# A graph network on one Trainium2 core: operands of VectorE moved to PSUM, the target comparison moved to ScalarE, and a memset behind each gather of GpSimd

## The chip, the core and the metric

The kernel is one program on one core of a Trainium2 chip. The metric is the device time of one execution in microseconds (us), the median of the runs shown. The profiled execution is a run of its own.

## What is computed

Two graph layers over 3125 nodes of 256 values and 53125 edges that are sorted by their target node (`dst`). Each layer is added to its input; each works on `h = relu(layernorm(x))`.

```
# first layer: attention over the edges, 4 heads of rank 16
ZU     = einsum('nd,kdr->knr', Z, U)
logits = (ZU[:, src] * ZU[:, dst]).sum(-1) / 4
exp_l  = exp(logits - segment_max(logits, dst)[dst])
alpha  = exp_l / (segment_sum(exp_l, dst)[dst] + 1e-16)
agg    = segment_sum(alpha[..., None] * ZU[:, src], dst)
ssa    = einsum('k,knr,kdr->nd', softmax(head_w), agg, U)
Z_half = 0.5 * Z + 0.5 * ssa
out    = relu(Z_half + 0.5 * ((Z_half - Z_half @ Dmat.T @ Dmat) @ Dmat) - 0.05)
# second layer: messages summed at their targets, then a GRU cell
red    = segment_sum(h[src] + relvectors[edge_type], dst)
out    = gru_cell(red, h)
```

## The kernel before

The nodes are cut into 25 windows of 125 (`NW`, `W`). The edges into one window lie together, and each window reads a span of 18 tiles of 128 edges (`C`), the edge on the partition. A set-up stage finds where each window's edges begin, makes ZU for all nodes and stores it as a table of 64 values a row in HBM (`zu_table`). The first layer then runs the windows one after another with the body of `attend` written out 25 times on each engine (`overlapped`); the second layer (`gru`) runs on the result and has no gather. The order on each engine is the order in which the code is written, and semaphores alone tie the engines together.

One window `t` of the first layer, `h = t % 2` being the half of each double buffer:

- **GpSimd** (`gather`, L638) fetches the source rows of ZU: 18 indirect DMAs, one for each tile of 128 edges, into `zs[h]`, in three chunks of 8, 8 and 2 tiles that count on semaphores of their own. The offsets are `sidx[:, h, :]`, which VectorE copied from `src_col` (`sources`, L963) once it was done with the same half two windows before. For the first two windows GpSimd copies them itself (L646).
- **SyncE** (`prefetch`) loads the targets of window `t + 2`, the same 2304 of them on each of 125 partitions, into `dst_bc[h]`, behind `oht_made`.
- **VectorE** multiplies the source rows with the target rows in PSUM (`logits`, L954) and sums over the rank (L957), chunk by chunk. Between the chunks it finishes the rows of window `t - 1`: `renew` (L1057 to L1066) and `shift` (L1071). Then it takes the maximum of each run of edges with the same target by two scans (L995, L997, L1001), makes the one-hots of the targets of window `t + 1` (`target_one_hots`, L924: `dst_bc` compared with the node number of the partition, written as bf16 to `ohT`), the remainder of the rows (L915), the difference of logits and maximum (`dif`, L1008), three bf16 parts of the target rows of `t + 1` (`split_rows`, L929 to L937), the weighted rows `V` (L1013: `zs` times the exponentials, both in SBUF), the offsets of window `t + 2` (L963), the cuts between runs (L941), the edge one-hots of `t + 1` (`one_hots`, L892: `iota_w` plus the window's first node compared with `dst_col`, both in SBUF) and a third of the finished rows (L919). When the sums of window `t` are there it divides by the denominators (`weigh`, L1038 on, whose instruction L1038 is the first of VectorE after TensorE's sums) and copies the transposed means (L1052).
- **ScalarE** does for window `t - 1` the logarithm and exponential of the layer norm, the rows `h2s` (L1404) and their first bf16 part (L1375), then for window `t` the copy of the transposed row (`keep_turned`, L1357), the exponential of `dif` straight into the columns `V[:, :, KR:KR + K]` (L1334, semaphore `P_made`), and afterwards the second bf16 part (L1380), the cuts (L1326), the counts (L1362) and the next dense row (L1352).
- **TensorE** transposes the logits (L1609) and the maxima (L1612), does a dense part (L1637), then makes the target rows of window `t + 1` from `ohT` and the three bf16 parts, 54 matmuls of 128x64 (`target_rows`, L1600), then the sums of window `t`, 18 fp32 matmuls (L1623, shown as 36), and last the transposed means and the product with them (L1641, L1643). `target_rows` waits for `oht_made` and for the five steps of `split_rows`.

Every engine has a second way through the kernel for graphs that do not fit the windows (`by_blocks`); it is not taken with these inputs and the change leaves it alone.

Of the kernel before, what the change touches and what calls it, by code (L numbers as in the profile page):

```python
# [24 lines left out]
def gnn_kernel(nc, x, edges, U, Dmat, head_w, rel, w_ih, w_hh, b_ih, b_hh, out):  # L25
# [5 lines left out]
    K, _, R = U.shape  # L31
    KR = K * R
# [23 lines left out]
    with ctx:  # L56
# [177 lines left out]
        any_top = sb("any_top", [W, 1])  # L234
        most_e = sb("most_e", [128, C * K])
# [127 lines left out]
        V_made = sem("V_made")  # L363
        agg_made = sem("agg_made")
# [9 lines left out]

        sidx_made = [sem(f"sidx_made{h}") for h in range(2)]
# [231 lines left out]
        def _(pool):  # L607
# [24 lines left out]
            def gather(i, h, table, to, done):  # L632

                pool.wait_ge(sidx_made[h], i + 1)
                pool.nop(nofuse=True)
                for c, (a, b) in enumerate(CHUNKS):
                    for j in range(a, b):
                        nc.gpsimd.indirect_dma_start(  # L638
                            out=to(h, j), out_offset=None, in_=table,
                            in_offset=bass.IndirectOffsetOnAxis(ap=sidx[:, h, j:j + 1], axis=0),  # L640
                        ).then_inc(done[h][c], 16)

            def windowed():
                pool.wait_ge(a_col, 1)
                for h in range(2):
                    nc.gpsimd.tensor_copy(sidx[:, h, :], src_col[:, h, :]).then_inc(sidx_made[h], 1)  # L646
                pool.wait_ge(st_zu, 16 * 5)
                each_window(lambda t, i, h: gather(
                    i, h, zu_table, lambda h, j: zs[h][:, j * KR:(j + 1) * KR], g_zs))
# [74 lines left out]
        def _(dve):  # L724
# [162 lines left out]
            def one_hots(t, h):  # L887

                in0 = iota_w[:, 0:W].unsqueeze(1).broadcast_to([128, C, W])
                col = flat(dst_col[:, :, :], t, C).unsqueeze(2).broadcast_to([128, C, W])  # L890
# [90 lines left out]
            def attend(t, i, h, first, last):  # L981
# [20 lines left out]
                ahead = (t + 1, i + h, 1 - h)  # L1002
                if not last:
                    target_one_hots(*ahead)
                if not first:
                    remainder(t - 1, 1 - h)
                dve.wait_ge(mT_made, t + 1)
# [805 lines left out]
```

## Time and profile before

| what | value |
|---|---|
| runs | 1218.30, 1241.45, 1218.26 us; median 1218.3 us |
| profiled execution | 1217.22 us, of which the profile's span is 1215.6 us |
| mean granted TensorE clock | 0.704 of full speed |
| busy in the span | PE 853.1 us (70%), DVE 682.5 us (56%), ACT 293.9 us (24%), POOL 563.5 us (46%) |
| 180 to 360 us | PE 118.59, DVE 108.06, ACT 27.85, POOL 142.82 us busy of 180; granted clock 0.50 |
| 405 to 760 us | PE 217.79, DVE 196.93, ACT 50.07, POOL 282.51 us busy of 355; granted clock 0.50 |

The span is that of one execution, from the first instruction to the last. PE is TensorE, DVE VectorE, ACT ScalarE, POOL GpSimd, SP SyncE. In a timeline each line gives the start, the duration, engine, line of the kernel, operation, tiles and shapes, and in brackets how long the engine sat idle before it and what ended that; "issue" is time in which it waited for nothing that the profile shows. The two stretches of the last two rows are both inside the windows of the first layer.

### The profile page before, as it was taken

The numbers are of one execution on the slowest core, as the hardware profiler recorded it, in microseconds if no ns is written. First come the engines' busy times: TensorE is split into PE (matmuls) and PEld (weight loads), VectorE is DVE, ScalarE is ACT, GpSimd is POOL, SyncE is SP. The second block draws the span as 40 slices with busy tenths as digits, with TensorE's granted clock in tenths as the row PEclk, the third lists the DMA queues.
The fourth block names the chain that finished last, engine by engine and source line by source line (L and its number), as shares of the span: only waits on it lengthen the run. The fifth ranks groups of instructions, "written<-read, shape, count | busy, mean of one in ns | idle before, by whom it ended". The sixth has DMA issues, their size and how long they took to land.

```text
span 1215.6 us, 14336 instructions
## 1 busy us (share of the span) xinstructions
PE 853.1 (70%) x5247; PEld 640.5 (53%) x5247; DVE 682.5 (56%) x1264; ACT 293.9 (24%) x621; POOL 563.5 (46%) x495
## 2 busy tenths in 40 slices
PE   0451656667655666665556666569999999999997
PEld 0341444456544455544445555446666666676764
DVE  4452566664565664455556555545566666555562
ACT  5230111111111111111111111224333333344331
POOL 3537277787778787777787877300000000000000
PEclk9985655555555555555555555569999999999999
DMA  4226233334333333332333331000000000000000
GB/s 126 79 48 128 81 72 69 73 79 95 73 70 71 73 81 82 78 68 68 71 71 74 80 84 35 12 13 18 17 15 16 13 18 17 18 17 18 18 14 14
DMA packets 42545, 65.97 MB, mean 54 GB/s; under 512 B 14247, under 2 KB 31696, under 8 KB 39350
## 3 DMA queue, kind: packets, MB, share of 16 engines
q1 hardware_dynamic: 24843, 48.23, 12.0%
q0 software_dynamic: 16576, 16.76, 11.0%
q8 instruction: 42, 0.69, 0.3%
q14 instruction: 28, 0.23, 0.1%
q10 hardware_dynamic: 1056, 0.07, 0.1%
HBM read 57.69 MB, written 7.20 MB: 53 GB/s over the span
## 4 chain that ended last, share of the span: by engine, by line
POOL 42%; PE 35%; issue 13%; DVE 4%; SPq 3%; DMA 2%; ACT 1%; POOLq 0%; DVEq 0%; ACTq 0%
POOL shared L638 40%; PE bank L1671 11%; PE bank L1670 5%; PE bank L1714 4%; PE bank L1721 4%; PE bank L1655 3%; PE bank L1722 2%; PE bank L1715 2%; DVE layer L1076 1%; DVE layer L1078 1%; POOL oh L712 1%; PE bank L1519 1%; PE bank L1682 1%; DMA layer<-in_edges,row_at 1%; DMA rels<-in_L_gnn_relvectors 1%
## 5 line engine op out<-in xcount | busy, mean ns | idle before, releaser
L638 POOL DMA_INDIRECT shared<-zu_table,sidx x450 | 534.5, 1188 | 162.9 <-issue 136.5
L1623 PE MATMUL bank<-layer,oh 128*125 128x84 f32 x900 | 192.1, 412 | 0.0
L1623 PEld LDWEIGHTS bank<-layer,oh 128*125 128x125 f32 x900 | 187.9, 326 | 0.0
L1600 PE MATMUL bank<-zu,shared 125*128 125x64 bf16 x1350 | 85.3, 238 | 78.8 <-issue 43.5
L1600 PEld LDWEIGHTS bank<-zu,shared 125*128 125x128 bf16 x1350 | 74.7, 127 | 102.4 <-issue 102.3
L1038 DVE TENSOR_SCALAR den<-bank 125x4 f32<-125x4 f32 x25 | 4.1, 162 | 189.9 <-issue 129.7
L1609 PE MATMUL bank<-ident,L 128*72 128x128 f32 x75 | 21.0, 417 | 125.6 <-DVE L L957 68.8
L1076 DVE COPY layer<-bank 125x256 f32<-125x256 f32 x25 | 10.6, 424 | 141.0 <-PE bank L1671 141.0
L907 DVE TENSOR_TENSOR shared<-iota_b,key_col 128x3125 bf16<-128x3125 bf16 x25 | 85.2, 3409 | 0.0
L907 DVE TENSOR_TENSOR oh<-iota_b,low_col 128x3125 bf16<-128x3125 bf16 x25 | 85.2, 3409 | 0.0
L1609 PEld LDWEIGHTS bank<-ident,L 128*72 128x72 f32 x75 | 9.4, 159 | 135.6 <-DVE L L957 73.8
L1362 ACT ACTIVATE cnt_rows<-meansT 51x125 bf16<-51x125 f32 x25 | 7.6, 305 | 281.7 <-issue 175.7
L1655 PEld LDWEIGHTS bank<-shared,oh 128*125 128x125 bf16 x625 | 61.7, 142 | 23.9 <-issue 10.0
L1655 PE MATMUL bank<-shared,oh 128*125 128x125 bf16 x625 | 66.5, 225 | 10.0 <-issue 9.0
L1671 PE MATMUL bank<-wide,zus 125*125 125x512 bf16 x208 | 73.3, 389 | 0.0
L1392 ACT ACTIVATE zus<-bank 125x500 bf16<-125x500 f32 (+1 forms) x91 | 60.3, 688 | 41.8 <-PE bank L1655 41.8
L1392 ACT ACTIVATE shared<-bank 125x500 bf16<-125x500 f32 (+1 forms) x84 | 55.8, 685 | 50.3 <-PE bank L1655 50.3
L1671 PE MATMUL bank<-wide,shared 125*125 125x512 bf16 x192 | 65.6, 379 | 0.0
L892 DVE SCALAR_TENSOR_TENSOR oh<-iota_w,win_first,dst_col 128x2250 f32<-128x2250 f32 x25 | 63.8, 2552 | 0.0
L954 DVE TENSOR_TENSOR layer<-shared,bank 128x512 f32<-128x512 f32 (+1 forms) x75 | 41.2, 549 | 37.1 <-DMA shared<-zu_table,sidx 33.3
L1670 PE MATMUL bank<-wide,zus 125*125 125x256 bf16 x195 | 54.3, 278 | 0.0
L1714 PE MATMUL bank<-whhT,layer 128*125 128x512 f32 x100 | 51.1, 593 | 0.0
(227 smaller groups left out, 1513.4 us busy)
## 6 DMA issues: line engine op xcount, KB each, us to landing
shared<-in_edges SPq DMA_DIRECT2D x25, 1125.0 KB
shared<-zu_table,sidx POOLq DMA_INDIRECT x450
xs<-in_x SPq DMA_DIRECT2D x5, 625.0 KB
h_table<-h2s SPq DMA_DIRECT2D x25, 125.0 KB
h2s<-h_table SPq DMA_DIRECT2D x25, 125.0 KB
out_dram<-layer SPq DMA_DIRECT2D x25, 125.0 KB
halo_i<-in_edges SPq DMA_DIRECT2D x25, 108.6 KB
zu_table<-zus SPq DMA_DIRECT2D x5, 156.2 KB
```

What stands on the lines that cost most here:

```text
L638: nc.gpsimd.indirect_dma_start(out=to(h, j), out_offset=None, in_=table, in_offset=bass.IndirectOffsetOnAxis(ap=sidx[:, h, j:j + 1], axis= ...
L892: nc.vector.scalar_tensor_tensor(o, in0, win_first[:, bass.ds(t, 1)], col, ALU.add, ALU.is_equal).then_inc(oh_made, 1)
L907: nc.vector.tensor_tensor(to.rearrange("p (g w) -> p g w", g=BW), io, col[:, t * BW:(t + 1) * BW].unsqueeze(2).broadcast_to([128, BW, W]), ...
L954: nc.vector.tensor_tensor(prod[:, a * KR:b * KR], zs[h][:, a * KR:b * KR], ps(c, 128, 0, (b - a) * KR), ALU.mult).then_inc(prod_made, 1)
L1392: nc.scalar.activation(many[t % 2].rearrange("p (a g d) -> p g a d", a=NW, g=BW)[:, a:b, :, :], ps((7, 1)[g % 2], W, 0, (b - a) * W).rearr ...
L1600: last = mm(ps(c, 128, (j - a) * KR, (j - a + 1) * KR), ohT[:, j * 128:(j + 1) * 128], zu3[:, m, :], start=m == 0, stop=m == 2)
L1623: last = mm(ps(5, W, 0, SUMS), oh[:, h, j * W:(j + 1) * W], V[:, j, :], start=j == 0, stop=j == C - 1)
L1655: last = mm(ps((7, 1)[g % 2], W, (k - a) * W, (k - a + 1) * W), lows[t % 2][:, k * W:(k + 1) * W], keys[t % 2][:, k * W:(k + 1) * W], star ...
L1670: mm(ps(0, W, 0, D), own, v[:, 2, :], start=False, stop=False)
L1671: last = mm(ps(0, W, 0, 2 * D), own, v[:, 0:2, :].rearrange("p m d -> p (m d)"), start=a == 0, stop=a == NW - 1)
L1714: mm(ps(rzb, W, 0, 2 * D), h2T[:, c * W:(c + 1) * W], whhT[:, c, 0:2 * D], start=False, stop=False)
L1721: mm(ps(rzb, W, 0, 2 * D), redT[:, c * W:(c + 1) * W], wihT[:, c, 0:2 * D], start=False, stop=c == CH - 1)
```

## The change

- The exponential of `dif` is made twice on ScalarE: first into PSUM (bank 4, columns 128 to 199), which VectorE's product L1013 now reads, then into `V` as before, for TensorE, under a new semaphore `P_kept`. VectorE's next `dif` and TensorE's sums wait for it.
- `one_hots` reads the targets of the window from PSUM (bank 3, columns 384 to 401), where ScalarE copies them (`targets`) after the exponentials. Window 0 still reads `dst_col` in SBUF.
- `target_one_hots` leaves VectorE. ScalarE makes it with two activations over 125x2304: the absolute difference of target and node, in place in `dst_bc`, and `relu(1 - that)` into `ohT`. In window `t` they stand behind `keep_turned(t)` and ahead of the exponentials.
- GpSimd takes the offsets from `src_col` directly; `sidx`, its semaphores, VectorE's copy L963 and GpSimd's two copies are gone from this way. Before the gathers of window `t` (from 2 on) it waits for `V` of window `t - 2`.
- Behind each gather GpSimd writes zeros to a tile of 128x64 (`idle`), which nothing reads; each of these memsets waits for the one before it.

```diff
+        idle = sb("idle", [128, 64])
...
-            def gather(i, h, table, to, done):
-
-                pool.wait_ge(sidx_made[h], i + 1)
-                pool.nop(nofuse=True)
+            def source_rows(t, i, h):
+
+                if t % GRP == 0:
+                    pool.wait_ge(a_col, 3 * (t // GRP) + 1)
+                if t >= 2:
+                    pool.wait_ge(V_made, t - 1 + CREDIT)
                 for c, (a, b) in enumerate(CHUNKS):
                     for j in range(a, b):
                         nc.gpsimd.indirect_dma_start(
-                            out=to(h, j), out_offset=None, in_=table,
-                            in_offset=bass.IndirectOffsetOnAxis(ap=sidx[:, h, j:j + 1], axis=0),
-                        ).then_inc(done[h][c], 16)
+                            out=zs[h][:, j * KR:(j + 1) * KR], out_offset=None, in_=zu_table,
+                            in_offset=bass.IndirectOffsetOnAxis(ap=src_col[:, t, j:j + 1], axis=0),
+                        ).then_inc(g_zs[h][c], 16)
+                        pool.wait_ge(c_pool, t * C + j + 1)
+                        nc.gpsimd.memset(idle[:, :], 0.0).then_inc(c_pool, 1)
...
             def one_hots(t, h):
-                col = flat(dst_col[:, :, :], t, C).unsqueeze(2).broadcast_to([128, C, W])
+                if t:
+                    dve.wait_ge(targets_made, t)
+                    col = ps(3, 128, 3 * 128, 3 * 128 + C)
+                else:
+                    col = dst_col[:, 0, :]
+                col = col.unsqueeze(2).broadcast_to([128, C, W])
...
-            def target_one_hots(t, i, h):
-                dve.wait_ge(l_bc[h], 16 * (i + 1))
-                nc.vector.tensor_scalar(ohT, dst_bc[h], node_id[0:W, bass.ds(t, 1)], None, ALU.is_equal).then_inc(oht_made, 1)
...
-            def sources(t, h):
-                dve.nop(nofuse=True)
-                nc.vector.tensor_copy(sidx[:, h, :], flat(src_col[:, :, :], t, C)).then_inc(sidx_made[h], 1)
...
                 dve.wait_ge(mT_made, t + 1)
+                if t:
+                    dve.wait_ge(P_kept, t)
                 nc.vector.tensor_tensor(dif[:, :], L[:, 1:C + 1, :].rearrange("p j k -> p (j k)"),
...
                                         zs[h].rearrange("p (j k r) -> p j k r", k=K, r=R),
-                                        V[:, :, KR:KR + K].unsqueeze(3).broadcast_to([128, C, K, R]),
+                                        ps(4, 128, 128, 128 + K * C).rearrange("p (j k) -> p j k", k=K)
+                                        .unsqueeze(3).broadcast_to([128, C, K, R]),
                                         ALU.mult).then_inc(V_made, 1)
...
                 keep_turned(t)
+                if not last:
+                    target_one_hots(t + 1, i + h, 1 - h)
                 act.wait_ge(dif_made, t + 1)
+                nc.scalar.activation(ps(4, 128, 128, 128 + K * C), dif[:, :], ACT.Exp, scale=float(R) ** -0.5).then_inc(P_made, 1)
                 nc.scalar.activation(V[:, :, KR:KR + K], dif[:, :].rearrange("p (j k) -> p j k", k=K), ACT.Exp,
-                                     scale=float(R) ** -0.5).then_inc(P_made, 1)
+                                     scale=float(R) ** -0.5).then_inc(P_kept, 1)
+                if not last:
+                    targets(t + 1)
...
+            def target_one_hots(t, i, h):
+
+                act.wait_ge(l_bc[h], 16 * (i + 1))
+                if t:
+                    act.wait_ge(zd_made[2], t)
+                away = dst_bc[h].bitcast(fp32)
+                nc.scalar.activation(away, dst_bc[h], ACT.Abs, bias=node_id[0:W, t:t + 1], scale=-1.0).then_inc(away_made, 1)
+                act.wait_ge(away_made, t + 1)
+                nc.scalar.activation(ohT, away, ACT.Relu, bias=ones[0:W, :], scale=-1.0).then_inc(oht_made, 1)
+
+            def targets(t):
+
+                nc.scalar.activation(ps(3, 128, 3 * 128, 3 * 128 + C), dst_col[:, t, :], ACT.Copy).then_inc(targets_made, 1)
...
                 pe.wait_ge(ohk_made, t + 1)
+                pe.wait_ge(P_kept, t + 1)
                 pe.wait_ge(V_made, t + 1 + CREDIT)
```

## Rows read from the trace of the kernel before

**Rows 1.** The page's chain that ended last, by line

```profile
POOL shared L638 40%; PE bank L1671 11%; PE bank L1670 5%; PE bank L1714 4%; PE bank L1721 4%; PE bank L1655 3%; PE bank L1722 2%; PE bank L1715 2%; DVE layer L1076 1%; DVE layer L1078 1%; POOL oh L712 1%; PE bank L1519 1%; PE bank L1682 1%; DMA layer<-in_edges,row_at 1%; DMA rels<-in_L_gnn_relvectors 1%
```

**Rows 2.** Groups by line and shape, 160 to 760 us: the gathers

```profile
L638 POOL DMA_INDIRECT shared<-zu_table,sidx x403 | 478.8, 1188 | 122.8 <-issue 122.8
```

**Rows 3.** Timeline of GpSimd: window 2's first gather, one late window, the last gather

```profile
148.63 2.98 POOL L638 DMA_INDIRECT shared<-zu_table,sidx  x1 [21.41 <-DVE sidx L963]
...
415.25 0.94 POOL L638 DMA_INDIRECT shared<-zu_table,sidx  x1 [0.30 <-issue]
...
419.00 0.94 POOL L638 DMA_INDIRECT shared<-zu_table,sidx  x1 [0.30 <-issue]
420.25 2.15 POOL L638 DMA_INDIRECT shared<-zu_table,sidx  x1 [0.30 <-issue]
...
423.97 1.95 POOL L638 DMA_INDIRECT shared<-zu_table,sidx  x1 [0.30 <-issue]
426.22 3.24 POOL L638 DMA_INDIRECT shared<-zu_table,sidx  x1 [0.30 <-issue]
...
453.26 3.24 POOL L638 DMA_INDIRECT shared<-zu_table,sidx  x1 [0.31 <-issue]
...
770.09 0.94 POOL L638 DMA_INDIRECT shared<-zu_table,sidx  x1 [0.30 <-issue]
```

**Rows 4.** Timeline of VectorE in the same stretch

```profile
415.14 0.69 DVE L954 TENSOR_TENSOR layer<-shared,bank 128x512 f32<-128x512 f32 x1 [1.65 <-DMA shared<-zu_table,sidx]
...
420.86 1.41 DVE L924 TENSOR_SCALAR shared<-shared,node_id 125x2304 bf16<-125x2304 int32 x1
...
423.75 1.35 DVE L1013 TENSOR_TENSOR layer<-shared,layer 128x1152 f32<-128x1152 f32 x1
...
425.76 2.55 DVE L892 SCALAR_TENSOR_TENSOR oh<-iota_w,win_first,dst_col 128x2250 f32<-128x2250 f32 x1
428.23 0.41 DVE L919 TENSOR_TENSOR wide<-rem,wide 125x256 bf16<-125x256 f32 x1
```

**Rows 5.** Timeline of VectorE: its first instruction behind TensorE's sums, windows 1, 8 and 23

```profile
181.29 0.16 DVE L1038 TENSOR_SCALAR den<-bank 125x4 f32<-125x4 f32 x1 [7.45 <-issue]
...
356.81 0.16 DVE L1038 TENSOR_SCALAR den<-bank 125x4 f32<-125x4 f32 x1 [7.97 <-issue]
...
759.40 0.16 DVE L1038 TENSOR_SCALAR den<-bank 125x4 f32<-125x4 f32 x1 [7.33 <-PE bank L1623]
```

**Rows 6.** Timeline of all engines inside one early window, 288 to 299 us

```profile
288.66 0.36 ACT L1357 ACTIVATE hTw_own<-bank 128x250 f32<-128x250 f32 x1
...
293.47 0.22 DVE L937 CAST zu<-rest 125x64 bf16<-125x64 f32 x1
293.61 1.34 DVE L1013 TENSOR_TENSOR layer<-shared,layer 128x1152 f32<-128x1152 f32 x1
...
293.84 1.86 PE L1600 MATMUL bank<-zu,shared 125*128 125x64 bf16 x32 [0.98 <-DVE zu L937]
...
298.69 1.54 PE L1623 MATMUL bank<-layer,oh 128*125 128x84 f32 x6
```

**Rows 7.** Groups by line and shape, 160 to 760 us: ScalarE

```profile
L1352 ACT ACTIVATE hrow_own<-xs,nmr,rstd 125x256 f32<-125x256 f32 x22 | 13.2, 601 | 0.6
...
L1326 ACT ACTIVATE cutf<-layer 72x385 f32<-72x385 f32 x23 | 12.1, 524 | 58.4 <-DVE layer L941 35.5 <-issue 22.9
...
L1380 ACT ACTIVATE wide<-rem 125x256 bf16<-125x256 f32 x16 | 6.4, 400 | 0.0
```

**Rows 8.** Timeline of GpSimd at the start of the kernel: memsets behind one another

```profile
1.69 0.09 POOL L618 MEMSET eps_col<- 128x1 f32 x1
1.73 2.70 POOL L620 MEMSET cnt_rows<- 115x3125 f32 x1
4.36 0.94 POOL L622 MEMSET wide<- 16x1024 f32 x1
```

**Rows 9.** Timeline of VectorE in the last window

```profile
773.57 0.29 DVE L954 TENSOR_TENSOR layer<-shared,bank 128x128 f32<-128x128 f32 x1 [1.52 <-DMA shared<-zu_table,sidx]
```

More of the change, by code:

```diff
@@ L363, in gnn_kernel @@
         V_made = sem("V_made")
+        P_kept = sem("P_kept")
+        away_made = sem("away_made")
+        targets_made = sem("targets_made")
         agg_made = sem("agg_made")
@@ L373, in gnn_kernel @@
         h2_made = sem("h2_made")
-        sidx_made = [sem(f"sidx_made{h}") for h in range(2)]
         red_made = sem("red_made")
@@ L638, in gather @@
                         nc.gpsimd.indirect_dma_start(
-                            out=to(h, j), out_offset=None, in_=table,
-                            in_offset=bass.IndirectOffsetOnAxis(ap=sidx[:, h, j:j + 1], axis=0),
-                        ).then_inc(done[h][c], 16)
+                            out=zs[h][:, j * KR:(j + 1) * KR], out_offset=None, in_=zu_table,
[3 more added lines that the diff above has]
+                        nc.gpsimd.memset(idle[:, :], 0.0).then_inc(c_pool, 1)
             def windowed():
-                pool.wait_ge(a_col, 1)
-                for h in range(2):
-                    nc.gpsimd.tensor_copy(sidx[:, h, :], src_col[:, h, :]).then_inc(sidx_made[h], 1)
                 pool.wait_ge(st_zu, 16 * 5)
-                each_window(lambda t, i, h: gather(
-                    i, h, zu_table, lambda h, j: zs[h][:, j * KR:(j + 1) * KR], g_zs))
+                each_window(source_rows)
             def block_gather(q, n, index, table, to):
@@ L1001, in attend @@
                 nc.vector.tensor_tensor(segmax[:, :], runs[:, 0, 128:256], runs[:, 1, 0:128], ALU.max).then_inc(segmax_made, 1)
-                ahead = (t + 1, i + h, 1 - h)
-                if not last:
-                    target_one_hots(*ahead)
                 if not first:
@@ L1014, in attend @@
                                         zs[h].rearrange("p (j k r) -> p j k r", k=K, r=R),
-                                        V[:, :, KR:KR + K].unsqueeze(3).broadcast_to([128, C, K, R]),
+                                        ps(4, 128, 128, 128 + K * C).rearrange("p (j k) -> p j k", k=K)
+                                        .unsqueeze(3).broadcast_to([128, C, K, R]),
                                         ALU.mult).then_inc(V_made, 1)
-                if t < NW - 2:
-                    dve.wait_ge(V_made, t + 1 + CREDIT)
-                    sources(t + 2, h)
                 if not last:
@@ L1099, in windowed @@
             def windowed():
-                target_one_hots(0, 0, 0)
                 split_rows(0)
@@ L1439, in windowed @@
             def windowed():
+                target_one_hots(0, 0, 0)
                 cuts(0, 0)
```

## The prediction

> **What bounds the kernel now.** I read the chain that ended last first: GpSimd's gathers, line 638, are 40% of it, and nearly all else in it is the second layer, which the change does not touch [rows 1]. The groups by line say how the gathers spend it: 403 of them in 160 to 760 us, 1.188 us each and 0.30 us between two (122.8/403), with nothing to wait for [rows 2].
>
> GpSimd's timeline then shows two kinds of gather. An undisturbed one takes 0.94 us and starts 1.247 us after the last; 18 of those are 22.45 us. In each late window three are longer: 2.15, 1.95 and 3.24 us [rows 3]. The same place comes back 27.04 us later (426.22 to 453.26), and 22.45 + 1.21 + 1.01 + 2.30 = 26.97, so these three are all of the difference. VectorE's timeline beside it names the causes [rows 4]. The 2.15 us gather ends at 422.40, just behind L924 (to 422.27). The 1.95 us gather starts under L1013 (to 425.10) and ends 0.82 us behind it; the 3.24 us gather starts under L892, L919 follows, and it ends (429.46) 0.82 us behind L919 (428.64). An instruction with one operand in PSUM does not do that: L954 runs from 415.14 to 415.83, a gather starts at 415.25 and takes 0.94 us.
>
> But the gathers are not the bound everywhere. I took the first VectorE instruction behind the sums of each window: from window 1 to window 8 it advances by 175.52 us, 25.07 a window, and from window 8 to window 23 by 402.59 us, 26.84 a window [rows 5]. GpSimd starts two windows ahead; while that lead lasts, VectorE never waits for a gather and the loop through VectorE, ScalarE and TensorE runs at its own 25.07 us. Only later does it wait for rows (1.65 us at 415.14 [rows 4]). So faster gathers can buy at most the way from 27 to that loop, and the loop is what has to be followed through the change.
>
> **The change part by part.** *The loop.* In an early window TensorE starts the target rows at 293.84, 0.15 us behind the last step of `split_rows` (293.69) [rows 6]. L924's 1.41 us leave VectorE ahead of it, so that step ends at about 292.3. The new one-hots are then late instead. ScalarE is free for them when L1357 ends, 289.02 [rows 6]. Their price is from rows of ScalarE [rows 7]: 256 elements without a pointer 0.400, 385 elements 0.524, and 256 with two pointers 0.601. The first two give 0.96 ns an element; with a fixed part of 0.19 and 0.84 ns an element both fit within 0.02, and a pointer is 0.10. So each is 0.19 + 0.10 + 2304 x 0.84 ns = 2.2 us (bounds 2.0, and 2.5 by the steeper slope). Two in a chain with 0.05 us of hand-over end at 289.02 + 4.45 = 293.47, and TensorE starts at 293.6, 0.25 us earlier than now. The exponential stands behind them on ScalarE: it ends near 293.75, so L1013 starts 0.1 us later than now and ends near 295.2; the sums come at 298.7 behind the target rows anyway [rows 6], so 3.5 us hide it. The second exponential, the copy of the targets and the wait for `P_kept` lie in the same 3.5 us. The loop becomes 25.07 - 0.25 = 24.8 us; bounds 24.2 (all of L924 but 0.5) and 25.4 (2.5 us an activation).
>
> *The gathers' stalls.* L924 is gone from VectorE, and L892 and L1013 each keep one operand in SBUF, as L954 has: 1.21 + 1.01 + 2.30 go. What can hit a gather in their place are the small instructions with both inputs in SBUF, of which L919 (0.41 us) is one; five such, each meeting the start of a gather about one time in three for half its length, are 0.4 us a window. I take 0.4 (bounds 0 and 1.5). The copy L963 goes from VectorE and was hidden under the sums; GpSimd's wait for it becomes one for V, right behind which the copy stood: nothing.
> Here the Trainium skill speaks both ways. By "SBUF — State Buffer", section "Who interferes with whom", a VectorE instruction with two SBUF inputs contends with a GpSimd instruction that reads SBUF, which the 1.95 us gather bears out; but the same section infers that a tensor_tensor does not hold up the generation of descriptors. If that held for these gathers, the moved operands would free nothing; it is a rival below.
>
> *The memset.* No memset stands beside a gather in this trace. At the start of the kernel the start of one follows that of the last by 0.04 us for one element (1.69 to 1.73) and 2.63 us for 3125 (1.73 to 4.36), so 0.84 ns an element [rows 8]: 64 elements are 0.05 + 0.04 = 0.09 us. It may cost more: handed over like a gather, with the 0.30 us that stand before each [rows 3], plus 0.15 of its own, it is 0.45. It may cost less than nothing, down to -0.30, if that gap is something that a following instruction fills. I take 0.09, since its kind has rows and they show no gap; its semaphore wait is for a memset that ended a whole gather before. Behind it in the queue stand the next gathers, and for them VectorE. The Trainium skill's "GPSIMD Engine Reference", section "Instruction dispatch", says that completion does not hold back the next GpSimd instruction; that speaks for the low end.
>
> *The sum.* Gathers: 22.45 + 18 x 0.09 + 0.4 = 24.5 us a window. From 148.6, where window 2's begin [rows 3], 23 windows end at 712. The loop: 181.3 + 22 x 24.8 = 727 at the place that is now 759.40 [rows 5], and the last window wants its last rows 14 us behind that (773.57 less 759.40 [rows 9]), at 741. The gathers are done 29 us before (now 2.5 us before, 771.0 [rows 3]): they no longer bind, the lead is never used up. Gain 759.4 - 726.9 = 32.5, plus the 1.52 us which the last window waits [rows 9], 34.0. The profiled execution would be 1217.2 - 34.0 = 1183.2; the median of the runs is 1.1 above it, so 1184.
>
> **The rivals.** *A, the memset is dear (slower).* Same mechanism, gathers as the bound. They bind once 23 windows end past 738, that is above 25.6 us a window, or 0.15 us a memset; at 0.23 they end at today's 771 and nothing is won; each 0.1 us beyond is 23 x 18 x 0.1 = 41 us. At 0.45 the window is 22.45 + 8.1 + 0.4 = 30.95 and the gathers end at 860: 1218.3 + 89 = 1307. For it: the gap of 0.30 before every gather is unexplained, and there is no row of a mix. Against it: the memsets' rows have no gap.
>
> *B, the stalls of L1013 and L892 stay* although an operand moves, as that inference has it. Then only L924's 1.21 goes: 27.0 - 1.2 + 1.6 = 27.4 a window, the gathers end at 148.6 + 23 x 27.4 = 779, 8 us later than now: 1226. Against it: L954's row. If only L892's 2.30 stayed, 24.5 + 2.3 = 26.8, an end at 765 and 1212.
>
> *C, ScalarE is the new late one*: at 3.0 us an activation, TensorE starts 1.35 us later than now, the loop is 26.4 and window 23's sums come at 181.3 + 22 x 26.4 = 762, so about 1219. For it: nothing on ScalarE runs beside these two, so all of their length counts. Against it: three shapes of rows agree on the slope.
>
> **How the numbers follow.** Forecast 0.58; A beyond 0.23 us 0.17; a memset between 0.15 and 0.23 us, or C, with 1195 to 1219, 0.13; B 0.12. 2% of 1218 is 24 us, about what a measurement of this kernel can tell from no change. The forecast's own range is 1170 (loop 24.2) to 1195 (loop 25.4); all of it counts as faster by over 2%, so faster 0.58. Same: B and the middle, and the near part of A, 0.26; slower 0.16. The range reaches from 1168 into the cases above: to 1232, which takes in B and A up to 0.28 us, and leaves some 0.14 above and 0.05 below.
>
> **What the profile after would show.** Right: gathers of 0.94 us even under the successors of L892 and L1013; starts of gathers 1.34 us apart; GpSimd waiting for VectorE once a window, VectorE not waiting for gathers in late windows; the loop at 24.8 us from window 1 to 23; ScalarE's two long activations 2.2 us each and TensorE's target rows released by ScalarE. Wrong: VectorE idle for DMA at the second and third chunk (A or B: the gathers' durations tell which, their spacing else), or activations near 3 us (C). A TensorE clock other than 0.5 in these stretches would void the loop's price.

## The result: 1319 us where 1184 was forecast, and 1135 us on chip 1

The changed kernel took 1319.19 us (median of 4 runs, 1318.62 to 1324.44), the kernel before 1218.28 us (4 runs): a ratio of 1.0824, 95% interval 1.0787 to 1.0861. The prediction was wrong, in size and in sign. The experiments add something that no profile of one kernel shows: the same changed kernel took 1309 and 1347 us on two other occasions, and **1134.81 us on chip 1**, a ratio of 0.9326 (0.9293 to 0.9359), where the kernel before took 1217.08. The median of the kernel before is within 3 us of 1218 beside every set of runs. Ratios and intervals are over fast runs alone, medians over all runs; where no ratio is given, the record has none.

The page of the changed kernel, chain that ended last, by engine and by line: beside [rows 1], the gathers' 40% are gone, and 17% stand under a releaser that the profile cannot name.

```profile
PE 39%; another core or an unknown queue 17%; DVE 17%; issue 15%; ACT 5%; SPq 3%; DMA 2%; POOL 1%; ACTq 0%; DVEq 0%
PE bank L1687 10%; PE bank L1686 5%; PE bank L1639 3%; PE bank L1730 3%; PE bank L1737 3%; PE bank L1671 3%; DVE oh L899 3%; PE bank L1615 2%; DVE layer L957 2%; ACT shared L1355 2%; ACT shared L1353 2%; PE bank L1738 2%; PE bank L1731 2%; DVE layer L1011 1%
```

There is one core only, so "another core" and "remote" mean that no recorded event explains the release. The page's groups say which instruction waits there: VectorE's first one behind the sums, L1034 (L1038 before, [rows 5]). GpSimd meanwhile waits for VectorE.

```profile
L642 POOL DMA_INDIRECT shared<-zu_table,src_col x450 | 439.2, 976 | 271.1 <-DVE layer L1011 187.3
L1034 DVE TENSOR_SCALAR den<-bank 125x4 f32<-125x4 f32 x25 | 4.1, 162 | 257.9 <-remote 231.1
...
L647 POOL MEMSET idle<- 128x64 f32 x450 | 77.0, 171 | 1.1 <-remote 0.9
```

The timeline of window 9, all engines, shows it in place (compare [rows 6]):

```profile
424.02 2.21 ACT L1355 ACTIVATE shared<-shared,ones 125x2304 bf16<-125x2304 f32 x1
...
426.30 2.35 PE L1615 MATMUL bank<-zu,shared 125*128 125x64 bf16 x54 [0.19 <-ACT shared L1355]
...
428.13 2.55 DVE L899 SCALAR_TENSOR_TENSOR oh<-iota_w,win_first,bank 128x2250 f32<-128x2250 f32 x1
...
428.48 4.14 PE L1639 MATMUL bank<-layer,oh 128*125 128x84 f32 x36
...
430.60 0.41 DVE L926 TENSOR_TENSOR wide<-rem,wide 125x256 bf16<-125x256 f32 x1
...
438.26 0.16 DVE L1034 TENSOR_SCALAR den<-bank 125x4 f32<-125x4 f32 x1 [7.24 <-remote]
```

The recorded sums end at 432.62; their result arrives at 438.26, 5.64 us late. I use this gap (end of the last recorded L1639 to the start of L1034), summed over windows 1 to 24, as the measure of lateness below: 175.8 us here, 0.9 us in the kernel before. The matmul records' ends are modelled, so TensorE can be slower than its rows say; in this window only the late result shows it, and further down are windows in which the rows show it too. A table by stretches (same window; columns: us, then busy us and count of PE, PE load, VectorE, ScalarE, GpSimd, then the granted clock, DMA share, GB/s) shows the clock going up, not down, for the sums, against a steady 0.5 in the kernel before:

```profile
421.00:426.20 5.20, 2.29 (x6) 1.26 (x5) 3.06 (x10) 4.66 (x4) 0.00 (x0) 0.50 0.17 42
426.30:428.40 2.10, 2.10 (x52) 2.10 (x53) 2.01 (x3) 0.81 (x5) 0.38 (x1) 0.67 0.46 92
428.40:432.60 4.20, 4.20 (x45) 4.07 (x41) 2.62 (x2) 0.37 (x1) 3.71 (x7) 1.00 0.55 151
432.60:438.20 5.60, 0.02 (x1) 0.00 (x0) 0.00 (x0) 0.00 (x0) 4.95 (x9) 0.67 0.33 102
```

Windows 2 to 22 take 26.6 to 34.3 us from L1034 to L1034, and from window 1 (193.48) to window 23 (862.51) one takes 30.4 us on average, not 24.8. So the stalls did go, and something worth more took their place: TensorE is held back by something other than the granted clock. I call it the hold.

### The profile page after: what moved, and what is told of

Same layout as the page of the kernel before. It is cut to its first block, busy times and chain, and to the rows that moved or that the text cites. A ratio compares the mean times of both kernels' runs of the same rounds, so it can differ in the third digit from the quotient of the medians.

```text
span 1316.8 us, 14863 instructions
## 1 busy us (share of the span) xinstructions
PE 764.1 (58%) x5247; PEld 561.5 (43%) x5247; DVE 644.7 (49%) x1216; ACT 407.8 (31%) x720; POOL 543.1 (41%) x943
## 4 chain that ended last, share of the span: by engine, by line
PE 39%; another core or an unknown queue 17%; DVE 17%; issue 15%; ACT 5%; SPq 3%; DMA 2%; POOL 1%; ACTq 0%; DVEq 0%
PE bank L1687 10%; PE bank L1686 5%; PE bank L1639 3%; PE bank L1730 3%; PE bank L1737 3%; PE bank L1671 3%; DVE oh L899 3%; PE bank L1615 2%; DVE layer L957 2%; ACT shared L1355 2%; ACT shared L1353 2%; PE bank L1738 2%; PE bank L1731 2%; DVE layer L1011 1%
## 5 line engine op out<-in xcount | busy, mean ns | idle before, releaser
L642 POOL DMA_INDIRECT shared<-zu_table,src_col x450 | 439.2, 976 | 271.1 <-DVE layer L1011 187.3
L1034 DVE TENSOR_SCALAR den<-bank 125x4 f32<-125x4 f32 x25 | 4.1, 162 | 257.9 <-remote 231.1
L1657 PE MATMUL bank<-ident,means 125*115 125x125 f32 x25 | 13.7, 547 | 200.7 <-DVE means L1041 106.0
L1639 PE MATMUL bank<-layer,oh 128*125 128x84 f32 x900 | 118.0, 296 | 0.0
L1639 PEld LDWEIGHTS bank<-layer,oh 128*125 128x125 f32 x900 | 114.9, 212 | 0.1
L1615 PE MATMUL bank<-zu,shared 125*128 125x64 bf16 x1350 | 71.2, 232 | 41.2 <-ACT shared L1355 33.9
L1657 PEld LDWEIGHTS bank<-ident,means 125*115 125x115 f32 x25 | 6.6, 263 | 204.7 <-DVE means L1041 108.2
L1615 PEld LDWEIGHTS bank<-zu,shared 125*128 125x128 bf16 x1350 | 68.1, 124 | 55.8 <-issue 41.6
L647 POOL MEMSET idle<- 128x64 f32 x450 | 77.0, 171 | 1.1 <-remote 0.9
L1627 PE MATMUL bank<-ident,segmax 72*128 72x72 f32 x25 | 9.4, 378 | 103.6 <-DVE segmax L1000 95.4
L899 DVE SCALAR_TENSOR_TENSOR oh<-iota_w,win_first,bank 128x2250 f32<-128x2250 f32 x24 | 61.1, 2548 | 0.0
```

Source lines behind the costliest of these rows:

```text
L642: nc.gpsimd.indirect_dma_start(out=zs[h][:, j * KR:(j + 1) * KR], out_offset=None, in_=zu_table, in_offset=bass.IndirectOffsetOnAxis(ap=sr ...
L647: nc.gpsimd.memset(idle[:, :], 0.0).then_inc(c_pool, 1)
L899: nc.vector.scalar_tensor_tensor(o, in0, win_first[:, bass.ds(t, 1)], col, ALU.add, ALU.is_equal).then_inc(oh_made, 1)
L1615: last = mm(ps(c, 128, (j - a) * KR, (j - a + 1) * KR), ohT[:, j * 128:(j + 1) * 128], zu3[:, m, :], start=m == 0, stop=m == 2)
L1639: last = mm(ps(5, W, 0, SUMS), oh[:, h, j * W:(j + 1) * W], V[:, j, :], start=j == 0, stop=j == C - 1)
```

## The experiments

Each is named with its chip's number (that of the result's own runs is not on record); times are medians, and the kernel before ran beside each.

**First set of runs, chip 0 (kernel before: 1220.28 us): which edit brings the hold?**

*The changed kernel without the memsets.*

```diff
-                        pool.wait_ge(c_pool, t * C + j + 1)
-                        nc.gpsimd.memset(idle[:, :], 0.0).then_inc(c_pool, 1)
```

> The changed kernel without the memsets. Theory M (the memsets make TensorE's results arrive late): the late arrivals are gone, from the start of the target rows to VectorE's first instruction behind the sums it is 6.6 to 12 us, and the time is 1180 to 1190 us, the forecast without its memset term. Theory S (the comparison on ScalarE lets TensorE's two long stages run as one burst, its granted clock goes up and something behind it slows): the late arrivals stay and the time is 1290 to 1320 us.

Measured: 1327.01 us (1304.31 to 1341.64, 4 runs), lateness 139.8 us. The memset is not the cause.

*The kernel before with the memset behind each gather, nothing else.*

> The kernel before with only the memset behind each gather. Theory M: TensorE's results arrive late here too, 3 to 11 us behind the sums, and the time is 1300 us or more. Theory S: no late arrival; the gathers stand 1.28 us apart instead of 1.25 with the stalls as before, 18 x 0.03 = 0.6 us a window more, 1230 us.

Measured: 1227.99 us (8 runs), ratio 1.0060 (1.0025 to 1.0095), lateness 0.9 us, windows of 27.3 us. A gather and its memset start 1.28 us after the last pair, 1.247 without: a memset costs 0.03 us, and 450 of them 14 us at most.

*The changed kernel with the target comparison back on VectorE* (operands in PSUM, offsets from the source table and the memset stay).

```diff
+            def target_one_hots(t, i, h):
+                dve.wait_ge(l_bc[h], 16 * (i + 1))
+                nc.vector.tensor_scalar(ohT, dst_bc[h], node_id[0:W, bass.ds(t, 1)], None, ALU.is_equal).then_inc(oht_made, 1)
```

> The changed kernel with the target comparison back on VectorE. Theory S: the late arrivals are gone, about 1190 us. Theory M: they stay, about 1310 us.

Measured: 1315.9 us (2 runs), ratio 1.0778 (1.0704 to 1.0852), lateness 143.8 us.

*The kernel before with only the comparison moved to ScalarE* (the two activations of the change; operands, offsets and gathers as before).

> The kernel before with only the target comparison moved to ScalarE. Theory S: late arrivals as in the changed kernel, 1290 us or more. Theory M: none; L924's stall of the gathers goes (1.2 us a window), so the gathers take 25.8 us a window and the time is about 1190 to 1200 us.

Measured: 1327.85 us (2 runs), ratio 1.0876 (1.0802 to 1.0949). Two versions that share no edited instruction both have the hold, so no one of the new instructions is needed for it. Here it takes another form: windows 3 to 23 are mostly quicker than before (18.4 to 25.5 us), but windows 2, 5, 8, 11, 15, 17 and 21 take 45 to 54 us. TensorE's timeline in window 2 shows it in the records themselves, at a granted clock of 0.5:

```profile
227.91 0.30 PE L1629 MATMUL bank<-layer,oh 128*125 128x84 f32 x1 [0.20 <-issue]
230.01 0.30 PE L1629 MATMUL bank<-layer,oh 128*125 128x84 f32 x1 [1.80 <-issue]
230.71 0.30 PE L1629 MATMUL bank<-layer,oh 128*125 128x84 f32 x1 [0.40 <-issue]
232.81 0.30 PE L1629 MATMUL bank<-layer,oh 128*125 128x84 f32 x1 [1.80 <-issue]
234.21 0.30 PE L1629 MATMUL bank<-layer,oh 128*125 128x84 f32 x1 [1.10 <-issue]
234.91 0.30 PE L1629 MATMUL bank<-layer,oh 128*125 128x84 f32 x1 [0.41 <-issue]
```

Single matmuls of 0.30 us start 2.10, 0.70, 2.10, 1.40 and 0.70 us apart: all multiples of 0.70 us, with nothing to wait for. The 36 matmuls of the sums take 23.65 us there, 7.83 in an ordinary window at the same clock. GpSimd's gathers beside them keep their 1.25 us.

In this window the steps end only when the gathers have ended. These are GpSimd's last two gathers of the window and TensorE's return to its ordinary pace 3.6 us behind that gather's end (233.42 to 237.04), with 11 of the 36 matmuls still to do:

```profile
231.22 0.94 POOL L639 DMA_INDIRECT shared<-zu_table,sidx  x1 [0.30 <-issue]
232.47 0.95 POOL L639 DMA_INDIRECT shared<-zu_table,sidx  x1 [0.30 <-issue]
...
236.31 0.30 PE L1629 MATMUL bank<-layer,oh 128*125 128x84 f32 x1 [1.10 <-issue]
237.04 2.57 PE L1629 MATMUL bank<-layer,oh 128*125 128x84 f32 x11 [0.43 <-issue]
```

The held traces of chip 0 have 12 windows in which 6 or more matmuls are left when the steps end (three each here, in the changed kernel and in the one-hots made twice of the third set, two without the memsets, one with the comparison on VectorE). In every one of them the steps end 2.2 to 5.4 us behind the end of the last gather. That speaks for the gathers as what holds TensorE there, since it is VectorE that GpSimd then waits for, and not TensorE directly. (In windows 8 and 11 here, with 3 and 1 left, the rows stop stepping earlier; the result comes 4.4 and 4.0 us behind the last gather.)

**Second set of runs, chip 7 (kernel before: 1217.02 us): what does the hold go with?**

*The memset made longer*, so that gathers start 1.49 us apart: `idle` of 320 elements instead of 64.

> The changed kernel with GpSimd's memset made longer (320 elements instead of 64), so that a gather and its memset take an estimated 1.5 us and the 18 of a window 27 us, the pace of the kernel before, still without any stalled gather. Theory R (TensorE is held back when its windows come faster than about every 27 us, whichever edit quickens them): the late arrivals of the sums go, from 231 us to under 20 us, and the time is 1225 to 1240 us. Theory C (one of the new instructions holds TensorE up, at any pace): still over 1290 us. Theory G (dense gathers hold TensorE up, by their DMA traffic or descriptor writing): between the two, as the gathers are only 15% sparser.

Measured: 1217.35 us, ratio 1.0009 (0.9993 to 1.0025), lateness 0.9 us.

*VectorE's one-hots made twice* (L899 doubled, 2.55 us more a window).

> The changed kernel with the one-hots of VectorE made twice, 2.55 us more of VectorE in each window; the gathers keep their spacing of 1.28 us. Theory R: VectorE now paces the window at an estimated 24.8 + 2.55 = 27.3 us, late arrivals under 20 us, time 1230 to 1250 us, less than the changed kernel's 1319 although work was added. Theories C and G: nothing that holds TensorE is taken away, so 1319 us or more, up to 2.55 us x 25 = 64 us more where VectorE's work does not lie beside the wait for the sums.

Measured: 1132.18 us, ratio 0.9318 (0.9264 to 0.9372), lateness 6.6 us, where VectorE itself comes late, as it waits for nothing in those windows: more work and 187 us less than the changed kernel had taken. It met no theory's number.

*One of three terms of the target rows* (36 of 54 matmuls of L1615 left out).

> The changed kernel with one of the three bf16 terms of the target rows: 36 of 54 matmuls of TensorE's target rows are left out in each window (the rows are rounded), nothing else changes. Theory R in the form that TensorE's own work per time is what brings the hold: late arrivals mostly go, windows of 21 to 24 us, time 1150 to 1200 us. Theory G: the late arrivals stay, as the gathers come as densely as before; only the 4.2 us of the left-out matmuls go, 1319 - 25 x 4.2 = 1215 us at the most favourable, and the sums still arrive over 5 us late in most windows.

Measured: 1135.67 us, ratio 0.9347 (0.9294 to 0.9399), lateness 0.9 us.

*Every second gather left out from window 2 on.*

> The changed kernel with every second gather left out from window 2 on (its slots keep the rows of two windows earlier), memsets unchanged: half the descriptor writing and half the gathers' DMA packets. Theory G: the late arrivals go, windows of 24.8 us or less, time 1160 to 1200 us. Theory R: TensorE, VectorE and ScalarE do the same work at the same or a faster pace, so the late arrivals stay: over 150 us in sum, time 1290 to 1340 us.

Measured: 1044.58 us, ratio 0.8597 (0.8549 to 0.8646), lateness 0.9 us, windows of 18.2 and 19.3 us in turn. All four are free of the hold, including three that took nothing from TensorE. Either each of four quite different edits cures it, or this chip does not have it; read alone, these runs would have seemed to speak for several theories at once.

**Third set of runs, chip 0 (kernel before: 1218.75 us): edit or chip?**

> The changed kernel once more, unchanged, beside the run with the one-hots made twice, both on one chip. That run took 1132 us on another chip than the one on which the changed kernel took 1319, so the two can differ by the chip or by the 2.55 us of VectorE. Theory D (dice: the hold of TensorE belongs to the chip or to the execution, and any version without the stalled gathers can have it or not): the changed kernel shows a time well under 1319 us here or in some of its executions, about 1130 us where no sum arrives late. Theory P (phase: the hold belongs to this order of the work and goes with a delay put into it): 1310 to 1330 us in every execution.

> The run with the one-hots made twice, repeated on the same chip as the changed kernel. Theory P: 1130 to 1136 us again, late arrivals under 10 us in sum, whatever the changed kernel shows beside it. Theory D: it takes the side that the changed kernel takes on this chip, 1320 us or more if the hold is there, 1130 us if not.

Measured: the changed kernel 1346.73 us (1333.92 to 1408.98, 4 runs), lateness 130.7 us; the one-hots made twice 1369.41 us (4 runs), ratio 1.1169 (1.1091 to 1.1247), lateness 174.4 us. The same file took 1132 us on chip 7 and 1369 on chip 0. Theory P falls.

The changed kernel shows both forms of the hold here in one trace. Its windows 2, 4 and 6 take 49.1 to 50.7 us, and TensorE's rows step by multiples of 0.70 us, in the target rows this time (window 2):

```profile
209.11 0.21 PE L1615 MATMUL bank<-zu,shared 125*128 125x64 bf16 x1 [1.89 <-issue]
209.83 0.21 PE L1615 MATMUL bank<-zu,shared 125*128 125x64 bf16 x1 [0.51 <-issue]
211.25 0.22 PE L1615 MATMUL bank<-zu,shared 125*128 125x64 bf16 x1 [1.20 <-issue]
```

From window 8 to 22 the rows look ordinary and the result comes 5.8 to 9.3 us late. That makes it likely that the two are one thing.

**Fourth set of runs, chip 5 (kernel before: 1219.34 us): the second set's variants beside the changed kernel.**

> The changed kernel unchanged, to show which kind of chip this call has. Theory D (the hold of TensorE belongs to the chip): about 1320 to 1350 us if the chip is one that holds TensorE back, 1130 to 1150 us if it is one that does not, and the other three runs of this call are read by that.

> The changed kernel with the memset lengthened so that a window's gathers take 27.1 us (as measured on the other chip, where it took 1217 us). On a holding chip, theory R (the hold comes when the windows are faster than about every 27 us): late arrivals under 20 us in sum, time 1217 to 1235 us, 90 to 100 us less than the changed kernel beside it. Theory K (the hold comes with the higher granted clock in TensorE's burst, whatever the pace): the clock still rises in most windows, so late arrivals over 100 us in sum and a time over 1290 us.

> The changed kernel with 36 of the 54 matmuls of the target rows left out per window. On a holding chip, theory W (the amount of TensorE's work per window brings the hold): late arrivals under 30 us in sum, time 1136 us as on the other chip. Theory R: the windows come every 21 to 24 us there, so the hold stays, over 100 us in sum, time over 1230 us.

> The changed kernel with every second gather left out from window 2 on. On a holding chip, theory G (gathers and their packets bring the hold): 1045 us as on the other chip. Theories R, K and W: the windows would come every 19 us with all of TensorE's work, so the hold is at least as hard as in the changed kernel: late arrivals over 130 us in sum, time 1280 to 1400 us.

Measured: the changed kernel 1309.02 us (1.0703; 1.0491 to 1.0914), lateness 169.6 us, so chip 5 holds. Gathers 1.49 us apart: 1217.95 us (0.9963; 0.9917 to 1.0008), lateness 44.6 us, hidden by VectorE's wait for rows. One term: 1338.02 us (1.0940; 1.0764 to 1.1116). Half the gathers: 1063.05 us (0.8692; 0.8513 to 0.8870), lateness 13.3 us. The stretch from 200 to 600 us (columns as above), first the changed kernel, then half the gathers:

```profile
200.00:600.00 400.00, 164.32 (x1422) 130.31 (x1423) 182.14 (x416) 110.94 (x187) 270.42 (x477) 0.61 0.26 68
```

```profile
200.00:600.00 400.00, 246.27 (x2089) 192.17 (x2089) 276.59 (x637) 168.71 (x286) 237.97 (x558) 0.67 0.35 87
```

With half the gathers, on the same chip in the same set of runs, TensorE does 2089 matmuls where the changed kernel does 1422, VectorE and ScalarE half as much again, DMA moves 87 GB/s instead of 68 and the clock is higher; and TensorE is hardly held. So neither the pace of the windows (R), nor the clock's rise (K), nor the amount of TensorE's work (W) brings the hold: it goes with the gathers (G). With the gathers 1.49 us apart GpSimd is busy for more of the stretch, 355.92 us, than in the changed kernel, and the hold is small:

```profile
200.00:600.00 400.00, 190.03 (x1550) 146.47 (x1550) 211.71 (x475) 125.73 (x212) 355.92 (x533) 0.63 0.34 75
```

This speaks for the gathers' spacing and against GpSimd's busy time as such. The run with one term denies W outright: with a third of the target rows' work, every second window takes 43.6 us and the one after it 21.4, at a clock of 0.5 throughout. Its lateness by my measure is only 3.4 us, since here the sums' own records are stretched. So the hold needs no rise of the clock either. The timeline of all engines in window 7 shows something more, in GpSimd's memsets:

```profile
366.24 0.30 PE L1638 MATMUL bank<-layer,oh 128*125 128x84 f32 x1 [1.80 <-issue]
366.28 0.15 POOL L647 MEMSET idle<- 128x64 f32 x1
366.58 0.95 POOL L642 DMA_INDIRECT shared<-zu_table,src_col  x1
...
368.34 0.30 PE L1638 MATMUL bank<-layer,oh 128*125 128x84 f32 x1 [1.80 <-issue]
368.37 0.15 POOL L647 MEMSET idle<- 128x64 f32 x1 [0.84 <-remote]
368.68 0.95 POOL L642 DMA_INDIRECT shared<-zu_table,src_col  x1 [0.15 <-issue]
...
369.74 0.30 PE L1638 MATMUL bank<-layer,oh 128*125 128x84 f32 x1 [1.10 <-issue]
369.78 0.15 POOL L647 MEMSET idle<- 128x64 f32 x1
...
373.27 0.30 PE L1638 MATMUL bank<-layer,oh 128*125 128x84 f32 x1 [1.62 <-issue]
373.30 0.15 POOL L647 MEMSET idle<- 128x64 f32 x1 [0.86 <-remote]
```

The memsets start 0.03 to 0.04 us behind TensorE's single matmuls, on the same steps of 0.70 us, and the gathers behind them come 2.1 and 1.4 us apart instead of 1.28. A memset waits for nothing but the semaphore of the one before it, whose work had ended long before (at 366.43 for the one that starts at 368.37). So in such a window the hold is not TensorE's alone: GpSimd's wait for its own semaphore is drawn out with it. VectorE and ScalarE keep the durations of their instructions (L899 2.55 us on chips 0, 1 and 5).

**Fifth set of runs, chip 1 (kernel before: 1217.08 us): the control is the finding.**

> The changed kernel unchanged, to show which kind of chip this call has: 1300 to 1350 us on one that holds TensorE back, 1125 to 1140 us (an estimate from the run with the one-hots made twice, 1132 us) on one that does not.

> Every second gather from window 2 on is replaced by a GpSimd memset of 1000 elements (an estimated 0.95 us, the length of a gather), so GpSimd is as busy as in the changed kernel and works 1.28 us per slot, while the gathers' DMA work is halved. On a holding chip, theory G (the gathers' descriptors and packets bring the hold): late arrivals under 30 us in sum, windows of 23 to 25 us, time 1130 to 1160 us. Theory B (GpSimd being busy beside TensorE brings it): late arrivals over 100 us, time over 1280 us. On a chip without hold both give about 1130 us.

> The changed kernel with a memset of 192 elements, by the two measured sizes (64: 0.17 us, 320: 0.38 us) 0.28 us, so a gather every 1.39 us and 25.0 us a window. If the hold falls evenly with the spacing (170 us of late arrivals at 1.28 us, 45 us at 1.49 us), late arrivals of about 105 us and a time near 1260 us on a holding chip; if it has a threshold below 1.39 us, under 50 us late and 1165 to 1180 us, which would beat both kernels there.

> The changed kernel with the long memset (0.38 us) behind the first 8 gathers of a window only, which run beside TensorE's target rows and sums where GpSimd waits for VectorE's V; the other 10 keep 1.28 us: 24.8 us a window. If only the gathers beside the burst matter, late arrivals under 50 us and 1165 to 1180 us on a holding chip; if their mean spacing matters, about 110 us late and 1260 us, as with the even memset of 192 elements.

Measured: the changed kernel 1134.81 us (0.9326; 0.9293 to 0.9359), half the gathers with GpSimd kept busy 1083.61 (0.8905; 0.8874 to 0.8937), the memset of 192 elements 1181.12 (0.9707; 0.9667 to 0.9746), the long memset behind eight gathers 1169.18 (0.9608; 0.9574 to 0.9643); lateness 0.9 us in each. Chip 1 does not hold, so the last three say nothing of the hold; they only show that, with all gathers made, the time follows their spacing (1181 at 1.39 us apart, between 1135 at 1.28 and 1217 at 1.49). No version tried that does all of the work beats the kernel before on a chip that holds; on chip 1 the changed kernel is the quickest of those that do (1134.81 us), and on chip 7 it was not run.

The changed kernel on chip 1, chain by line, and its groups from 160 to 760 us:

```profile
POOL shared L642 36%; PE bank L1687 12%; POOL idle L647 6%; PE bank L1686 6%; PE bank L1730 4%; PE bank L1737 4%; PE bank L1671 3%; PE bank L1738 2%; PE bank L1731 2%; SPq L505 1%; DVE layer L1072 1%; DVE layer L1074 1%; POOL oh L714 1%; PE bank L1534 1%; PE bank L1698 1%
```

```profile
L642 POOL DMA_INDIRECT shared<-zu_table,src_col x404 | 397.1, 983 | 66.5 <-issue 66.5
...
L647 POOL MEMSET idle<- 128x64 f32 x404 | 67.8, 168 | 0.2
...
L957 DVE TENSOR_TENSOR layer<-shared,bank 128x512 f32<-128x512 f32 x46 | 31.5, 684 | 82.5 <-DMA shared<-zu_table,src_col 82.3
...
L1034 DVE TENSOR_SCALAR den<-bank 125x4 f32<-125x4 f32 x24 | 3.9, 162 | 71.2 <-PE bank L1639 71.2
```

The same view of the changed kernel in the profile of the result:

```profile
L642 POOL DMA_INDIRECT shared<-zu_table,src_col x353 | 343.3, 972 | 198.3 <-DVE layer L1011 143.8 <-issue 54.5
...
L957 DVE TENSOR_TENSOR layer<-shared,bank 128x512 f32<-128x512 f32 x40 | 27.3, 682 | 0.3 <-issue 0.3
...
L1034 DVE TENSOR_SCALAR den<-bank 125x4 f32<-125x4 f32 x20 | 3.2, 162 | 213.1 <-remote 199.5 <-issue 13.6
```

Without the hold nothing is "remote", GpSimd never waits, and VectorE waits for rows. One window on chip 1, GpSimd and then the other engines:

```profile
386.95 0.95 POOL L642 DMA_INDIRECT shared<-zu_table,src_col  x1 [0.16 <-issue]
...
388.23 1.10 POOL L642 DMA_INDIRECT shared<-zu_table,src_col  x1 [0.16 <-issue]
...
389.66 0.95 POOL L642 DMA_INDIRECT shared<-zu_table,src_col  x1 [0.16 <-issue]
...
390.94 1.20 POOL L642 DMA_INDIRECT shared<-zu_table,src_col  x1 [0.16 <-issue]
...
392.47 0.95 POOL L642 DMA_INDIRECT shared<-zu_table,src_col  x1 [0.16 <-issue]
```

```profile
386.91 2.57 PE L1615 MATMUL bank<-zu,shared 125*128 125x64 bf16 x54
389.32 4.14 PE L1639 MATMUL bank<-layer,oh 128*125 128x84 f32 x36
```

```profile
386.69 1.35 DVE L1011 TENSOR_TENSOR layer<-shared,bank 128x1152 f32<-128x1152 f32 x1
...
388.43 2.55 DVE L899 SCALAR_TENSOR_TENSOR oh<-iota_w,win_first,bank 128x2250 f32<-128x2250 f32 x1
...
393.49 0.16 DVE L1034 TENSOR_SCALAR den<-bank 125x4 f32<-125x4 f32 x1 [2.18 <-PE bank L1639]
```

The recorded sums are the same 4.14 us as in the held window 9; here they end at 393.46 and the result is there at 393.49. The records of TensorE's work do not tell the two windows apart; the consumer does.

Two more things on record set the two kinds of chip apart. The kernel before takes 1217 to 1220 us on all of them, but its mean granted clock is 0.699 to 0.715 on chips 0 and 5 (and 0.704 in the profile before the change) and 0.746 to 0.763 on chips 1 and 7. And the traces differ in what they kept: for the same 14863 instructions the result's trace has 5060 recorded semaphore updates and chip 1's has 12082, with an update for every instruction that makes one. Every trace of chips 0 and 5 lacks some of these, that of the kernel before with memsets too (5951), and so does the kernel before's own trace (5433); no trace of chips 1 and 7 does.

## Why the prediction was wrong, step by step

**The stalls go: right.** On chip 1 the 3.24 us gather beside the one-hots is 1.10 now and the one beside L1011 0.95; a gather is 972 ns on average in 160 to 760 us instead of 1188 [rows 2]. What was left over is 1.10 and 1.20 where 0.95 stands elsewhere, together the 0.4 us a window that I took. The Trainium skill's "SBUF — State Buffer", "Who interferes with whom", holds for its contention rule; its inference that a tensor_tensor leaves the generation of descriptors alone does not hold here, since the 1.01 us went when one operand of L1013 (L1011 now) moved.

**The memset: nearly right.** 0.03 us a gather where I took 0.09: the memset is 0.17 us long, but the idle time before the next gather falls from 0.30 to 0.16 us. Rival A falls. By the Trainium skill's "GPSIMD Engine Reference", "Instruction dispatch", completion does not hold back the next instruction; the rows agree: in the held window above the gather at 366.58 starts 0.15 us behind the memset of 366.28, while the next memset, which waits for that one's semaphore, starts only at 368.37, after 0.84 us of idling.

**The gathers' window: near.** 18 x 1.28 + 0.4 = 23.4 us; on chip 1 it is 23.6 (393.49 to 417.09), I had 24.5. Rival B falls.

**ScalarE's activations: right.** 2.20 and 2.22 us for 2.2 (means of L1353 and L1355, 160 to 760 us); TensorE's target rows are released by L1355. Rival C falls.

**The loop, 24.8 us a window: the step that failed, in both directions.** It was priced from rows at a clock of 0.5 and took it for granted that TensorE runs at that clock and that it does what its rows say.
- *Upward, on every chip:* in the changed kernel the clock rises to 1.0 for 6.8 us in most windows (18 of them between 160 and 760 us in the result's profile, 23 on chip 1; none in the profile before). The pace of the windows is not what lifts it: with the long memset on chip 7 it rises 18 times too, and windows 5 to 7, of 27.1 us each, have a mean clock of 0.62. No run separates which part of the change does. Target rows and sums then take 6.8 us from first matmul to L1034 (410.27 to 417.09) against 10.7 at 0.5 (paced run, windows 20 to 22). With every second gather away the loop runs in 18.2 to 19.3 us. So where nothing holds TensorE, the gathers stay the bound, as they were, and the gain is all that they give: window 23's L1034 moves from 759.40 [rows 5] to 675.71, 83.7 us earlier; I had moved it to 727, 32.5 earlier. The change itself is worth 82.3 us there (1217.08 - 1134.81), below the low end of my range. From window 1 to 23 a window takes 22.8 us there (173.93 to 675.71) where I had 24.8, and my conclusion that the gathers would no longer bind fails with it.
- *Downward, on some chips:* the hold. In the result's profile window 23's L1034 comes at 862.51, 103.1 us later than before; 175.8 us of late sums, and smaller delays of the transposes (41.2 us of "remote" before the scans, L994, in 160 to 760 us), outweigh what the clock gives. At a clock of 0.5 and without hold my figure is about what was measured: windows 14 and 20 with only the comparison moved, both at a mean clock of 0.50, took 25.3 and 25.5 us.

The prediction's last sentence named another clock as what would void the price of the loop, but gave it no chance and no number. And no rival had TensorE itself in it. All three looked at the edited instructions. One bound of the prediction was added up wrongly: the loop at 25.4 us is 22 x 0.6 = 13.2 us above the forecast, 1197 and not 1195, and neither is over 2% below 1218; nothing above turns on it.

**Shown:** TensorE is held, in its own rows where they step by 0.70 us, and drawn-out semaphore waits of GpSimd go with it; no single edit is needed for it. The changed kernel was held on chips 0 and 5 and free on 1, and four variants were free on 7. Only chip 0 was used twice, held both times; for the others "the chip" could also be the occasion. On chip 5 the hold nearly goes with half the gathers, at the highest pace of everything else, and shrinks when they are 1.49 us apart; on chip 0 the steps end 2.2 to 5.4 us behind the last gather.

**Not shown:** why the kernel before is spared. I took it that its stalled gathers (2.15, 1.95 and 3.24 us, [rows 3]) fall just beside TensorE's burst and thin them out there. The record speaks against the largest of them: with only the comparison moved, the 3.24 us gather stands beside TensorE's burst in the held windows as well (in window 2 it starts at 206.41, while the target rows already step). The run meant for this question (the long memset behind eight gathers) landed on a chip without hold.

**Open:** what differs between the chips; whether the gathers' descriptors, their packets or their semaphore updates matter, for the first two of which the run with GpSimd kept busy was meant; what the 0.70 us step is. An untested rival is the recording itself: every run on record has a recorded span and clock, and the traces of the chips that hold lack semaphore updates, so it is not shown that an execution nobody records is held. Against recording alone as the cause: the kernel before loses updates as well (5433 kept) and is not held. Queues that bring instructions are an unlikely cause: the busier of the two moves the same 42 packets (0.69 MB) on chip 1 as in the result's profile.

## What to carry to other kernels

Work that comes faster once a stall is gone can meet an engine that does not keep up: before pricing a faster loop, give the engine beside it, its clock included, a rival of its own. When a result arrives later than its producer's recorded end and the releaser is "remote" on a single core, measure the producer by its consumer. And before explaining a slowdown, run the unchanged pair on a second chip: the result's four runs agreed within 0.5% here, and still told only half of it; every set of experiments needs the disputed kernel itself as a control.

## What the hardware showed that I had not expected

- One kernel on one core takes 1134.81 us on chip 1, 1309.02 on chip 5 and 1346.73 on chip 0, while another kernel of the same work takes 1217 to 1220 on all of them, at a mean granted clock of 0.75 on chip 1 and 0.70 on chips 0 and 5.
- TensorE can be held far below its granted clock: 36 matmuls in 23.65 us instead of 7.83, single ones starting in multiples of 0.70 us, while the gathers beside them keep their 1.25 us. Where GpSimd waits for a semaphore of its own in such a window, that wait is drawn out on the same steps (memsets at 366.28, 368.37 and 369.78 behind matmuls at 366.24, 368.34 and 369.74).
- The hold goes with the indirect gathers: on chip 5 lateness 169.6 us at 1.28 us apart, 44.6 us at 1.49, 13.3 us with every second gather left out; on chip 0 TensorE is back at its pace 2.2 to 5.4 us behind the last gather.
- A GpSimd memset of 64 elements behind a gather costs 0.03 us, as it fills the gap before the next one.
